# Two half-precision parts, one bias pass, and waits of GpSimd for VectorE's router operations

## The chip, the core and the metric

The kernel runs on one core of a Trainium2 chip. The core has TensorE (PE in the profile), VectorE (DVE), ScalarE (ACT), GpSimd (POOL) and SyncE (SP), each with its own instruction queue; they synchronize by semaphores. The metric is the device time of one launch in microseconds (us), the median over runs.

## What is computed

The input `x` is 16 images of 64 channels and 112x112 pixels, in f32. Cut to what matters:

```python
n  = layernorm over channels of x                     # per pixel
y  = sigmoid(conv3x3([max_c n, mean_c n]) + conv_b)   # one gate per pixel
x1 = x + n * y
t  = tokens of x1 (one per pixel, 64 values)
z  = layernorm(t)
p  = softmax(z @ router_w + router_b)                 # 8 experts
top_p, top_i = top_k(p, 2); top_p /= top_p.sum()
out = t + sum_k top_p[k] * (z @ expert_w[top_i[k]] + expert_b[top_i[k]])
```

The router bias and the expert biases are not zero in the inputs that are run.

## The kernel before, in words

Images go in 8 pairs (two images of 64 channels fill the 128 partitions). A pair has 14 steps of 8 image rows (896 pixels of each image). Three stages are software-pipelined over pairs: in a *round* r, stage A centres pair r and collects its channel maximum and sum of squares; stage B computes the square roots, the 3x3 convolution and the router for pair r-1; stage C applies the experts to pair r-2, with a lag of two steps. Rounds 2 to 7 have all three stages, round 8 has no A, rounds 9 and 10 have C alone. All queues are unrolled and written out by hand; each engine runs its own in order.

In C, the 18 numbers of a token (8 gates, 8 scaled gates, and two affine terms) lie in `q`. They must go through TensorE to be spread over channels, and TensorE reads them in bf16, so they are cut into three bf16 parts: ScalarE rounds `q` to the first (`part_one`), GpSimd subtracts it (`rest_one`), ScalarE rounds the rest to the second (`part_two`), and GpSimd subtracts again for the third (`part_three`). TensorE turns the parts (`turn`, L458), ScalarE copies the result to `s`. TensorE then spreads gates from `s` into PSUM `gb` (`spread`, L465) and the affine term into `tm` (`spread_a1`, L504), starts each of two accumulations `moe` with the biases (`biases`, L514: a pass with the high half `bh` of the bias, one with the low half `bl`), and adds the eight expert products (`experts`, L520). In each step six of eight gate multiplications are VectorE's (`scale_unit`, L662, reading PSUM) and two are GpSimd's (L1148, reading a copy that ScalarE made, L963). VectorE also adds `x1` (`finish`, L675); GpSimd forms it (`scale_x`, L1173).

VectorE's part of B is cut in *places*, two a step: place 2*step at the step's start, place 2*step+1 after the first half's work (`gate`). Places 1 to 3 and 7 to 9 hold Newton steps of the roots, 4 and 6 the convolution's input and the affine terms, 12 to 19 the router of the first half of the pixels, 20 to 27 that of the second. GpSimd has its part of B (`router`, `router_tail`) at a fixed point of each step, after `rest_one`. A *half step* below is one of the two halves that the queues of TensorE and VectorE are written in, each with one call of `biases`, three `scale_unit` on VectorE, one `finish` and, in rounds with A, one `channel_max` and one `centre_rows`.

Of the kernel before, what the change touches and what calls it, by code (L numbers as in the profile page):

```python
# [26 lines left out]
BF16 = mybir.dt.bfloat16  # L27
# [6 lines left out]
E = 8  # L34
P = 128
# [20 lines left out]
SR = SB + 3 * QN  # L56
QG, QB, QA, QM = 0, E, 2 * E, 2 * E + 1
# [13 lines left out]
B_POOL = ("lg_0", "bias_0", "lg_1", "bias_1", "m1_0", "m2_0", "qb_0", "qg_0", "m1_1", "m2_1", "qb_1", "qg_1")  # L71
# [4 lines left out]

def constant_arrays():

    f = np.zeros((P, CC + 3 * W + E + P), np.float32)
# [12 lines left out]
    f[:, o:o + E] = np.arange(E, 0, -1)  # L92
    o += E
    for part in range(3):
        for b in range(2):
            f[b * SB + part * QN + QM, o + b * CH:o + (b + 1) * CH] = -1.0
    g = np.zeros((P, (KT + 2) * P), np.float32)
    for part in range(3):
        for b in range(2):
            row = b * SB + part * QN  # L100
            for k in range(KT):
                for e in range(2):
                    lo = k * P + e * CH
                    g[row + QG + 2 * k + e, lo:lo + CH] = 1.0
            g[row + QA, KT * P + b * CH:KT * P + (b + 1) * CH] = 1.0
    g[:, (KT + 1) * P:] = np.eye(P)
    return f, g


def gated_expert_program(nc, x, conv_w, conv_b, router_w, router_b, expert_w, expert_b, const_f, const_g, out):  # L110
# [3 lines left out]
    with ExitStack() as ctx:  # L114
# [9 lines left out]
        cf = sb("cf", [P, CC + 3 * W + E + P])  # L124
        cg = sb("cg", [P, (KT + 2) * P], BF16)
# [9 lines left out]
        bias_base = cf[0:SR, bias_c:bias_c + P]  # L135

# [7 lines left out]
        bl = sb("bl", [SR, P], F16)  # L144
# [41 lines left out]
        res = sb("res", [W, 2, ROWS, 2 * QN])  # L186
        parts = sb("parts", [W, 2, ROWS, 2 * SB], BF16)
        s = sb("s", [P, 2, TOK], BF16)
# [11 lines left out]
        turn_out = tm[:, 1, :].bitcast(BF16)  # L200
# [25 lines left out]
        part2 = sem("part2")  # L226
        part3 = sem("part3")
# [13 lines left out]
        FIRST_LOADS, LOADS, BIAS_LOADS = 3 * 16, 5 * 16, 6 * 16  # L241
        POOL_SETUP = 5 + 1 + 6 * 5 + 1 + 2
# [71 lines left out]
        def part_of(v, n):  # L314

            return parts[:, v % 2, :, :].rearrange("w j (b k) -> w j b k", b=2)[:, :, :, n * QN:(n + 1) * QN]

        def by_part(t):
            return t.rearrange("w j (b k) -> w j b k", b=2)
# [14 lines left out]
        def _(sp):  # L334
# [66 lines left out]
            for part in range(3):  # L401
                for b in range(2):
                    row = b * SB + part * QN + QB
                    col = bias_c + b * CH
                    sp.dma_start(cf[row:row + E, col:col + CH], expert_b).then_inc(ld_bias, 16)
# [13 lines left out]
        def _(pe):  # L419
# [29 lines left out]
            def turn(r, step, v):  # L449

                if due(count := c_at(r, 1, v, 1)):
                    pe.wait_ge(part3, count)
                read_out(pe, r, step, 0)
                if due(count := c_at(r, 1, v - 1, 1)):
                    pe.wait_ge(a1_out, count)
                for j in range(ROWS):
                    for b in range(2):
                        last = pe.transpose(turn_out[b * SB:(b + 1) * SB, j * W:(j + 1) * W],  # L458
                                            parts[:, v % 2, j, b * SB:(b + 1) * SB], ident)
                last.then_inc(turned, 1)  # L460

            def spread(v, k, c, slot):
                for b in range(2):
                    rows = slice(b * SB, b * SB + 3 * QN)
# [44 lines left out]
            def biases(r, v, c):  # L509
                if due(count := c_at(r, 2, v - 1, c + 1)):  # L510
                    pe.wait_ge(final, count)
                for n, w in enumerate((bh, bl)):
                    for b in range(2):
                        pe.matmul(moe[b * CH:(b + 1) * CH, c, 0:HALF], w[:, b * CH:(b + 1) * CH],  # L514
                                  s[0:SR, v % 2, c * HALF:(c + 1) * HALF],
                                  start=(n == 0), stop=False, skip_group_check=True)
# [364 lines left out]
        def _(act):  # L881
# [168 lines left out]
            def body(r, A, Bp, steps=STEPS, tail=True):  # L1050
                for step in range(steps):
# [28 lines left out]
                    if parting:  # L1080
                        part_two(r, v + 2)
# [22 lines left out]
        def _(pool):  # L1104
# [26 lines left out]
            link(pool.tensor_tensor(bl[:, :], bias_base, bh[:, :], ALU.subtract))  # L1131
# [195 lines left out]
```

## Time and profile before

| | |
|---|---|
| median of 3 runs | 1491.57 us (1489.61 to 1493.1) |
| profiled execution | 1497.93 us, span 1496.1 us |
| busy in the span | TensorE 94%, VectorE 85%, GpSimd 73%, ScalarE 72% |
| mean granted TensorE clock | 0.963 of full |
| matmuls of the bias passes (L514) | 896 |
| all matmuls | 12198 |

The table is read from the profiled execution: the span runs from the first to the last instruction, and busy time is that in which an engine has an instruction in execution. A granted clock of 1.00 is TensorE's 2.4 GHz, 0.50 is 1.2 GHz.

### The profile page before, as it was taken

To read this page: it belongs to the slowest core of one execution; us is meant where nothing else is said; L and a number is where in the kernel's file an instruction comes from. 1 tells how busy PE (TensorE), PEld (TensorE's weight loads), DVE (VectorE), ACT (ScalarE), POOL (GpSimd) and SP (SyncE) were. 2 spreads that over 40 slices of the span, in tenths; PEclk is the share of its full clock that TensorE was granted. 3 is DMA by queue.
4 is the path that set the end of the run, shared out by engine and by line. 5 is a ranking of instruction groups with operands and counts; after the bars stand their busy time and mean duration, and the time that the engine had idled before them with its cause. 6 is when DMAs were issued, how large, how long until landed. Compare 5 with 4: busy or idle time off the path is not lost.

```text
span 1496.1 us, 34317 instructions
## 1 busy us (share of the span) xinstructions
PE 1402.2 (94%) x12198; PEld 660.5 (44%) x12198; DVE 1268.4 (85%) x1583; ACT 1080.0 (72%) x4061; POOL 1086.4 (73%) x729
## 2 busy tenths in 40 slices
PE   8854999999999999999999999999999889999998
PEld 8853444444444444444444444444444233333332
DVE  6787889988998889988898889988898788977776
ACT  6667788878887888878888788878888334444432
POOL 5234687868777787877788687876878678887765
PEclk9955999999999999999999999999999899999999
DMA  6442466656666566666656666666665356556563
GB/s 221 125 114 60 138 197 197 203 156 203 190 188 193 178 199 197 185 179 193 185 173 198 186 186 192 177 199 186 195 193 169 101 151 170 173 164 182 165 181 112
DMA packets 85851, 260.04 MB, mean 174 GB/s; under 512 B 13744, under 2 KB 13744, under 8 KB 85680
## 3 DMA queue, kind: packets, MB, share of 16 engines
q1 hardware_dynamic: 85680, 257.85, 57.7%
q8 instruction: 97, 1.59, 0.4%
q14 instruction: 74, 0.61, 0.1%
HBM read 206.41 MB, written 51.38 MB: 172 GB/s over the span
## 4 chain that ended last, share of the span: by engine, by line
PE 69%; DVE 9%; issue 7%; POOL 3%; ACT 3%; DVEq 0%; POOLq 0%; ACTq 0%
PE moe L520 39%; PE gb L465 13%; PE tm L444 8%; DVE gx L662 7%; PE moe L514 4%; PE tm L458 3%; PE tm L504 2%; POOL gx L1148 1%; PE tm L544 1%; POOL tt L1173 1%; ACT a1s L970 1%; ACT sq L919 1%; POOL parts L1162 1%; DVE stats L639 0%; ACT logit_mean L985 0%
## 5 line engine op out<-in xcount | busy, mean ns | idle before, releaser
L662 DVE TENSOR_TENSOR gx<-gb,xd 128x896 f32<-128x896 f32 x672 | 710.7, 1085 | 139.0 <-PE gb L465 135.6
L520 PE MATMUL moe<-gx,wc 128*64 128x448 f32 x3584 | 820.6, 558 | 0.0
L1148 POOL TENSOR_TENSOR gx<-gs,xd 128x896 f32<-128x896 f32 x224 | 486.2, 2170 | 302.1 <-ACT gs L963 291.6
L963 ACT ACTIVATE gs<-gb 128x896 f32<-128x896 f32 x224 | 205.3, 917 | 225.1 <-PE gb L465 225.0
L919 ACT ACTIVATE sq<-xct 112x64 f32<-112x64 f32 x1400 | 338.0, 244 | 8.1 <-DVE early_s L649 2.6
L520 PEld LDWEIGHTS moe<-gx,wc 128*64 128x64 f32 x3584 | 219.2, 137 | 244.0 <-issue 193.3
L465 PE MATMUL gb<-s,cg 54*128 54x448 bf16 x1792 | 261.4, 360 | 40.8 <-DVE gx L662 34.6
L919 ACT ACTIVATION_READ_ACCUMULATOR sq<-xct 112x1 f32 x1400 | 263.7, 188 | 0.0
L1173 POOL TENSOR_TENSOR tt<-xc,a1s 128x896 f32<-128x896 f32 x112 | 236.2, 2109 | 12.2 <-issue 10.5
L465 PEld LDWEIGHTS gb<-s,cg 54*128 54x128 bf16 x1792 | 57.0, 95 | 377.9 <-DVE gx L662 292.6
L444 PEld LDWEIGHTS tm<-rhs,xa 64*112 64x112 f32 x2800 | 175.1, 185 | 29.7 <-issue 11.5
L444 PE MATMUL tm<-rhs,xa 64*112 64x74 f32 x2800 | 171.7, 265 | 11.2 <-ACT logit_mean L904 8.4
L675 DVE TENSOR_TENSOR ot<-moe,tt 128x448 f32<-128x448 f32 x224 | 138.0, 616 | 31.5 <-PE moe L520 30.8
L900 ACT ACTIVATE xct<-tm 112x512 f32<-112x512 f32 x175 | 104.2, 595 | 61.2 <-PE tm L444 55.6
L970 ACT ACTIVATE a1s<-tm,ones 128x896 f32<-128x896 f32 x112 | 112.8, 1007 | 43.5 <-PE tm L504 43.5
L955 ACT ACTIVATE s<-tm 128x896 bf16<-128x896 bf16 x112 | 102.6, 916 | 11.9 <-PE tm L458 7.2
L639 DVE TENSOR_REDUCE stats<-xct 112x8 f32<-112x512 f32 x128 | 86.8, 678 | 18.3 <-ACT logit_mean L904 17.5
L1156 POOL TENSOR_TENSOR res<-q,parts 112x288 f32<-112x288 f32 x112 | 81.2, 725 | 9.7 <-ACT parts L942 9.7
L458 PEld LDWEIGHTS tm<-cg,parts 112*64 112x64 bf16 x1792 | 56.8, 111 | 67.7 <-POOL parts L1162 44.1
L1162 POOL TENSOR_TENSOR parts<-res,parts 112x288 bf16<-112x288 f32 x112 | 83.1, 742 | 0.1
L514 PE MATMUL moe<-s,bh 118*64 118x448 bf16 x448 | 80.8, 354 | 0.0
L639 DVE TENSOR_REDUCE early_s<-xct 112x8 f32<-112x512 f32 x96 | 65.1, 678 | 18.2 <-ACT early_l L904 17.3
(94 smaller groups left out, 1296.7 us busy)
## 6 DMA issues: line engine op xcount, KB each, us to landing
xd<-in_x_dram SPq DMA_DIRECT2D x448, 224.0 KB, 4.0
xa<-in_x_dram SPq DMA_DIRECT2D x112, 448.0 KB, 4.3
xc<-in_x_dram SPq DMA_DIRECT2D x112, 448.0 KB, 4.8
out_dram<-ot SPq DMA_DIRECT2D x112, 448.0 KB, 3.3
gx<-in_const_g_dram SPq DMA_DIRECT2D x1, 384.0 KB, 4.7
cf<-in_const_f_dram SPq DMA_DIRECT2D x1, 332.5 KB, 2.8
gx<-in_L_ffn_expert_w_dram SPq DMA_DIRECT2D x1, 128.0 KB, 4.5
cf<-in_L_ffn_expert_b_dram SPq DMA_DIRECT2D x6, 2.0 KB
```

Source lines behind the costliest of these rows:

```text
L444: last = pe.matmul(pair[:, b, j, :], xa[chans, step % XA, row * W:(row + 1) * W], rhs1[chans, :], start=True, stop=True)
L465: last = pe.matmul(gb[:, 2 * slot + b, 0:HALF], cg[rows, k * P:(k + 1) * P], s[rows, v % 2, c * HALF:(c + 1) * HALF], start=True, stop=True)
L514: pe.matmul(moe[b * CH:(b + 1) * CH, c, 0:HALF], w[:, b * CH:(b + 1) * CH], s[0:SR, v % 2, c * HALF:(c + 1) * HALF], start=(n == 0), stop= ...
L520: last = pe.matmul(moe[b * CH:(b + 1) * CH, c, 0:HALF], wc[:, k * CH:(k + 1) * CH], gx[:, u, b, :], start=False, stop=(k == KT - 1), skip_ ...
L639: dve.tensor_reduce(to[:, 0, lo + cols.start:lo + cols.stop], xct[:, step % 2, cols, :], AX.X, ALU.max) \
L662: dve.tensor_tensor(gx[:, i, :, :], gb[:, 2 * slot:2 * slot + 2, 0:HALF], xd[:, v % 2, :, c * HALF:(c + 1) * HALF], ALU.mult).then_inc(sca ...
L675: dve.tensor_tensor(ot[:, sl, cols], moe[:, c, 0:HALF], tt[:, sl, cols], ALU.add).then_inc(final, 1)
L919: last = act.activation(sq[:, n, :], xct[:, step % 2, n, :], ACT.Square, accum_out=to[:, 1, lo + n:lo + n + 1])
L963: act.activation(gs[:, j, :, :], gb[:, 2:4, 0:HALF], ACT.Copy).then_inc(gate_out, 1)
L970: act.activation(a1s[:, v % 2, :].rearrange("p (c t) -> p c t", c=2), tm[:, :, 0:HALF], ACT.Identity, bias=ones[:, :], scale=1.0).then_inc ...
L1148: pool.tensor_tensor(gx[:, ND + j, :, :], gs[:, j, :, :], xd[:, v % 2, :, j * HALF:(j + 1) * HALF], ALU.mult).then_inc(scaled_p, 1)
L1173: pool.tensor_tensor(tt[:, sl, :], xc[:, sl, :], a1s[:, sl, :], ALU.mult).then_inc(scaled_x, 1)
```

## The change

`q` is cut in two f16 parts instead of three bf16 parts: ScalarE's `part_one` and GpSimd's `rest_one` remain, `part_two` and `part_three` go. The 18 columns of a token are written out as two overlapping blocks of 13 columns (the eight gates and what follows them appear in both), so that a part has 26 rows and each gate stands twice; the bias matrix `bw` holds the high half of the bias at one copy of a gate and the low half at the other, so one pass of `biases` does what two did. GpSimd's scaled gates are written in two instructions, of 5 and 3 columns. GpSimd gets two more setup instructions and SyncE two more small bias loads. And ahead of each of its gate multiplications GpSimd waits until VectorE has ended the last operation of that half step's place (`vector_place`), where there is one.

```diff
 QN = 2 * E + 2
 SB = 64
-SR = SB + 3 * QN
-QG, QB, QA, QM = 0, E, 2 * E, 2 * E + 1
+G_LO = 5
+QB, QA, QM = G_LO, 2 * E, 2 * E + 1
+BLOCK, AGAIN = QB + E, QB
+PN = 2 * BLOCK
+SR = SB + 2 * PN
 D_PAIR = (0, 1, 3, 0, 1, 3)
 P_PAIR = 2
...
+        PLACE_END = {1: "y_a1", 2: "y_b1", 3: "r1", 4: "pool_mean", 6: "v2", 7: "y_a2", 8: "y_b2", 9: "rho"}
+        HALF_END = ("top", "ge", "key_max", "dl", "d", "ge2", "key_max2", "oh2")
+        for place in range(16):
+            PLACE_END[12 + place] = f"{HALF_END[place % 8]}_{place // 8}"
+
+        def vector_place(eng, r, place):
+
+            if 1 <= r <= PAIRS and place in PLACE_END:
+                b_done(eng, r, B_DVE, PLACE_END[place])
...
-            return parts[:, v % 2, :, :].rearrange("w j (b k) -> w j b k", b=2)[:, :, :, n * QN:(n + 1) * QN]
-
-        def by_part(t):
-            return t.rearrange("w j (b k) -> w j b k", b=2)
+            tokens = parts[:, v % 2, :, :].rearrange("w j (b k) -> w (j b) k", b=2)
+            return tokens[:, :, n * PN:(n + 1) * PN].rearrange("w t (i k) -> w t i k", i=2)
+
+        def q_blocks(v):
+
+            rows = q[:, v * ROWS:(v + 1) * ROWS, :]
+            return bass.AP(rows.tensor, rows.offset, [rows.ap[0], [QN, 2 * ROWS], [AGAIN, 2], [1, BLOCK]])
...
             def turn(r, step, v):
 
                 if due(count := c_at(r, 1, v, 1)):
-                    pe.wait_ge(part3, count)
+                    pe.wait_ge(rest1, count)
...
-                for n, w in enumerate((bh, bl)):
-                    for b in range(2):
-                        pe.matmul(moe[b * CH:(b + 1) * CH, c, 0:HALF], w[:, b * CH:(b + 1) * CH],
-                                  s[0:SR, v % 2, c * HALF:(c + 1) * HALF],
-                                  start=(n == 0), stop=False, skip_group_check=True)
+                for b in range(2):
+                    pe.matmul(moe[b * CH:(b + 1) * CH, c, 0:HALF], bw[:, b * CH:(b + 1) * CH],
+                              s[0:SR, v % 2, c * HALF:(c + 1) * HALF],
+                              start=True, stop=False, skip_group_check=True)
...
-                act.activation(part_of(v, 0), by_part(q[:, v * ROWS:(v + 1) * ROWS, :]), ACT.Copy) \
-                   .then_inc(part1, 1)
-
-            def part_two(r, v):
-                if due(count := c_at(r, 1, v, 1)):
-                    act.wait_ge(rest1, count)
-                act.activation(part_of(v, 1), by_part(res[:, v % 2, :, :]), ACT.Copy).then_inc(part2, 1)
...
-                    if parting:
-                        part_two(r, v + 2)
...
-            link(pool.tensor_tensor(bl[:, :], bias_base, bh[:, :], ALU.subtract))
+            link(pool.tensor_tensor(bias_base, bias_base, low_row.to_broadcast([SR, P]), ALU.mult))
+            link(pool.tensor_tensor(bh[:, :], bh[:, :], high_sign.to_broadcast([SR, P]), ALU.mult))
+            link(pool.tensor_tensor(bw[:, :], bias_base, bh[:, :], ALU.add))
...
             def rest_one(r, v):
                 if due(count := c_at(r, 1, v, 1)):
                     pool.wait_ge(part1, count)
-                if due(count := c_at(r, 1, v - 2, 1)):
-                    pool.wait_ge(part3, count)
-                pool.tensor_tensor(by_part(res[:, v % 2, :, :]), by_part(q[:, v * ROWS:(v + 1) * ROWS, :]),
-                                   part_of(v, 0), ALU.subtract).then_inc(rest1, 1)
-
-            def part_three(r, v):
-                if due(count := c_at(r, 1, v, 1)):
-                    pool.wait_ge(part2, count)
-                pool.tensor_tensor(part_of(v, 2), by_part(res[:, v % 2, :, :]),
-                                   part_of(v, 1), ALU.subtract).then_inc(part3, 1)
...
-                pool.tensor_tensor(q_tokens[:, rows, QG:QG + E], q_tokens[:, rows, QB:QB + E], wide(rho, rows),
+                rhos = wide(rho, rows)
+                pool.tensor_tensor(q_tokens[:, rows, 0:G_LO], q_tokens[:, rows, QB:QB + G_LO], rhos[:, :, 0:G_LO],
                                    ALU.mult).then_inc(b_pool, 1)
+                pool.tensor_tensor(q_tokens[:, rows, QB + E:QA], q_tokens[:, rows, QB + G_LO:QB + E],
+                                   rhos[:, :, G_LO:E], ALU.mult).then_inc(b_pool, 1)
...
                     cur, ahead, parting = on(r, v), on(r, v + 1), on(r, v + 2)
                     if cur:
+                        vector_place(pool, r, 2 * step)
                         scale_unit(r, v, 1)
                     if parting:
                         rest_one(r, v + 2)
@@ -1286,10 +1305,9 @@
                     if Bp:
                         router(r, step)
                     if ahead:
+                        vector_place(pool, r, 2 * step + 1)
                         scale_unit(r, v + 1, 0)
                         scale_x(r, v + 1)
-                    if parting:
-                        part_three(r, v + 2)
```

GpSimd's queue in rounds with all stages, from the multiplication at the start of step 0 to `scale_x` of that step and what follows (`gx<-gs,xd` is a gate multiplication, `tt<-xc,a1s` is `scale_x`, `e<-stats` feeds the first root; `b_dve` counts VectorE's operations of B). Before:

```order
L1148 TENSOR_TENSOR gx<-gs,xd 128x896 [waits mixed,gate_out]
L1156 TENSOR_TENSOR res<-q,parts 112x288 [waits part3,part1]
L1207 TENSOR_TENSOR dl<-oh,g 112x896 [waits b_act,b_dve]
L1237 TENSOR_TENSOR e<-stats,powers 112x224 [waits b_dve,joined,squared]
L1148 TENSOR_TENSOR gx<-gs,xd 128x896 [waits mixed,gate_out,ld_xd1]
L1173 TENSOR_TENSOR tt<-xc,a1s 128x896 [waits final,a1_out,ld_xc1]
L1162 TENSOR_TENSOR parts<-res,parts 112x16x18 [waits part2]
```

After:

```order
L1172 TENSOR_TENSOR gx<-gs,xd 128x896 [waits mixed,gate_out]
L1178 TENSOR_TENSOR parts<-q,parts 112x16x26 [waits part1]
L1222 TENSOR_TENSOR dl<-oh,g 112x896 [waits b_act,b_dve]
L1255 TENSOR_TENSOR e<-stats,powers 112x224 [waits b_dve,joined,squared]
L1172 TENSOR_TENSOR gx<-gs,xd 128x896 [waits gate_out,mixed,ld_xd1,b_dve]
L1188 TENSOR_TENSOR tt<-xc,a1s 128x896 [waits final,a1_out,ld_xc1]
```

The subtraction into `res` became one into `parts`, the second subtraction (`part_three`) is gone, and the multiplication behind `e<-stats` waits for `b_dve` too. The other multiplications behind a place of VectorE wait alike.

TensorE's queue in the second half of a step, with the two bias passes between the turned affine term and the expert products. The piece before:

```order
L504 MATMUL tm<-s,cg 64x448 x4
L514 MATMUL moe<-s,bh 64x448 x2
L514 MATMUL moe<-s,bl 64x448 x2
L520 MATMUL moe<-gx,wc 64x448 x2
L465 MATMUL gb<-s,cg 128x448 x4
L444 MATMUL tm<-rhs,xa 112x74 x8
```

and after:

```order
L535 MATMUL tm<-s,cg 64x448 x4
L544 MATMUL moe<-s,bw 64x448 x2
L550 MATMUL moe<-gx,wc 64x448 x2
L496 MATMUL gb<-s,cg 128x448 x4
L475 MATMUL tm<-rhs,xa 112x74 x8
```

Two of the four bias matmuls of a half step are gone; the rest keeps its order.

## Rows read from the trace of the kernel before

**Rows 1.** The page's busy time, share of the span and instructions of each engine.
```profile
PE 1402.2 (94%) x12198; PEld 660.5 (44%) x12198; DVE 1268.4 (85%) x1583; ACT 1080.0 (72%) x4061; POOL 1086.4 (73%) x729
```

**Rows 2.** Timeline of TensorE, 466 to 483, first bias pass: start, duration (us), line.
```profile
466.84 0.36 PE L514 MATMUL moe<-s,bh 118*64 118x448 bf16 x2
...
472.63 0.36 PE L514 MATMUL moe<-s,bh 118*64 118x448 bf16 x2
...
482.48 0.36 PE L514 MATMUL moe<-s,bh 118*64 118x448 bf16 x2
```

**Rows 3.** The chain of waits, 634 to 640: start, duration, what.
```profile
638.58 0.38 PE moe L514 x4
```

**Rows 4.** Groups by line and shape: busy us, mean ns | idle before, releaser.
```profile
L1173 POOL TENSOR_TENSOR tt<-xc,a1s 128x896 f32<-128x896 f32 x112 | 236.2, 2109 | 12.2 <-issue 10.5 <-ACT a1s L970 1.7
...
L1162 POOL TENSOR_TENSOR parts<-res,parts 112x288 bf16<-112x288 f32 x112 | 83.1, 742 | 0.1
L1156 POOL TENSOR_TENSOR res<-q,parts 112x288 f32<-112x288 f32 x112 | 81.2, 725 | 9.7 <-ACT parts L942 9.7
...
L948 ACT ACTIVATE parts<-res 112x288 bf16<-112x288 f32 x112 | 48.3, 431 | 0.0
```

**Rows 5.** Timeline, 577 to 584: a half step with place 18, and GpSimd beside it.
```profile
577.30 0.73 POOL L1162 TENSOR_TENSOR parts<-res,parts 112x288 bf16<-112x288 f32 x1
...
577.40 1.10 DVE L689 TENSOR_TENSOR key<-ge,prio 112x896 bf16<-112x896 bf16 x1
...
578.54 1.09 DVE L681 TENSOR_REDUCE key_max<-key 112x112 bf16<-112x896 bf16 x1
...
579.55 1.08 DVE L662 TENSOR_TENSOR gx<-gb,xd 128x896 f32<-128x896 f32 x1
...
583.69 0.61 DVE L714 TENSOR_TENSOR oh<-prio,ge 112x896 bf16<-112x896 bf16 x1
```

**Rows 6.** One line's instructions: duration ns min/median/max, first and last start.
```profile
L662 DVE TENSOR_TENSOR gx<-gb,xd x672: 1071/1083/1093, 144.2 to 1490.1; 128x896 f32<-128x896 f32 x168
```

**Rows 7.** Timeline, 643 to 648: step 0 of a round with all stages.
```profile
643.38 0.28 DVE L745 TENSOR_SCALAR p<-e 112x224 int32<-112x224 int32 x1 [0.65 <-POOL e L1237]
...
644.12 0.39 DVE L753 SCALAR_TENSOR_TENSOR u<-u,e 112x224 f32<-112x224 f32 x1
644.18 2.33 POOL L1148 TENSOR_TENSOR gx<-gs,xd 128x896 f32<-128x896 f32 x1 [0.84 <-issue]
...
644.55 2.21 DVE L756 SCALAR_TENSOR_TENSOR p<-u,p 112x224 f32<-112x224 f32 x1
...
647.82 0.93 PE L465 MATMUL gb<-s,cg 54*128 54x448 bf16 x4 [2.31 <-DVE gx L662]
```

**Rows 8.** Busy (count) of PE, PEld, DVE, ACT, POOL in two stretches; granted clock, DMA.
```profile
648.00:655.00 7.00, 7.00 (x36) 3.06 (x34) 5.24 (x8) 2.52 (x11) 1.38 (x2) 0.53 0.54 132
1200.00:1210.00 10.00, 7.82 (x48) 2.47 (x46) 9.63 (x14) 2.26 (x3) 5.94 (x5) 1.00 0.40 123
```

**Rows 9.** Timelines of VectorE and TensorE, 1154 to 1240, in round 8.
```profile
1160.25 2.22 DVE L753 SCALAR_TENSOR_TENSOR u<-u,e 112x224 f32<-112x224 f32 x1
...
1177.01 2.25 DVE L756 SCALAR_TENSOR_TENSOR r<-u,p 112x224 f32<-112x224 f32 x1
...
1202.16 0.55 PE L465 MATMUL gb<-s,cg 54*128 54x448 bf16 x4 [2.04 <-DVE gx L662]
...
1211.55 2.31 DVE L756 SCALAR_TENSOR_TENSOR p<-u,p 112x224 f32<-112x224 f32 x1
```

**Rows 10.** Timelines of GpSimd and VectorE, 602 to 609: step 11 of a round.
```profile
602.56 2.14 POOL L1148 TENSOR_TENSOR gx<-gs,xd 128x896 f32<-128x896 f32 x1 [0.86 <-ACT gs L963]
...
605.33 2.11 POOL L1216 TENSOR_TENSOR q<-lg,dl 112x896 f32<-112x896 f32 x1
...
607.36 0.61 DVE L697 TENSOR_TENSOR oh<-prio,ge 112x896 bf16<-112x896 bf16 x1
...
608.01 1.09 DVE L699 SCALAR_TENSOR_TENSOR dl<-oh,lg 112x896 f32<-112x896 bf16 x1
```

More of the change, by code:

```diff
@@ L70 @@
          + tuple(n + "_1" for n in HALF_ROUTER))
-B_POOL = ("lg_0", "bias_0", "lg_1", "bias_1", "m1_0", "m2_0", "qb_0", "qg_0", "m1_1", "m2_1", "qb_1", "qg_1")
+B_POOL = ("lg_0", "bias_0", "lg_1", "bias_1", "m1_0", "m2_0", "qb_0", "ql_0", "qg_0", "m1_1", "m2_1", "qb_1",
+          "ql_1", "qg_1")
 B_NORM = ("e1", "e2")
@@ L74, with gate_col, part_col @@
 GUESS = 0x5F3759DF
+def gate_col(e):
+    return e if e < G_LO else E + e
+def part_col(col):
+    return col if col < AGAIN else BLOCK + col - AGAIN
 def constant_arrays():
-    f = np.zeros((P, CC + 3 * W + E + P), np.float32)
+    f = np.zeros((P, CC + 3 * W + E + P + 2), np.float32)
     for b in range(2):
@@ L93, in constant_arrays @@
     o += E
-    for part in range(3):
+    f[:, o + P] = 1.0
+    for part in range(2):
         for b in range(2):
-            f[b * SB + part * QN + QM, o + b * CH:o + (b + 1) * CH] = -1.0
+            row = b * SB + part * PN
+            f[row + part_col(QM), o + b * CH:o + (b + 1) * CH] = -1.0
+            low = slice(row + part_col(QB), row + part_col(QB) + E)
+            f[low, o + P], f[low, o + P + 1] = -1.0, 1.0
     g = np.zeros((P, (KT + 2) * P), np.float32)
-    for part in range(3):
+    for part in range(2):
         for b in range(2):
-            row = b * SB + part * QN
+            row = b * SB + part * PN
             for k in range(KT):
@@ L103, in constant_arrays @@
                     lo = k * P + e * CH
-                    g[row + QG + 2 * k + e, lo:lo + CH] = 1.0
-            g[row + QA, KT * P + b * CH:KT * P + (b + 1) * CH] = 1.0
+                    g[row + part_col(gate_col(2 * k + e)), lo:lo + CH] = 1.0
+            g[row + part_col(QA), KT * P + b * CH:KT * P + (b + 1) * CH] = 1.0
     g[:, (KT + 1) * P:] = np.eye(P)
@@ L122, in sem @@
             return ctx.enter_context(nc.semaphore(name))
-        cf = sb("cf", [P, CC + 3 * W + E + P])
-        cg = sb("cg", [P, (KT + 2) * P], BF16)
+        cf = sb("cf", [P, CC + 3 * W + E + P + 2])
+        cg = sb("cg", [P, (KT + 2) * P], F16)
         gx = sb("gx", [P, UNITS, 2, HALF])
@@ L135, in gated_expert_program @@
         bias_base = cf[0:SR, bias_c:bias_c + P]
+        high_sign = cf[0:SR, bias_c + P:bias_c + P + 1]
+        low_row = cf[0:SR, bias_c + P + 1:bias_c + P + 2]
         cg_load = gx_flat[:, 0:(KT + 2) * P]
@@ L143, in gated_expert_program @@
         bh = sb("bh", [SR, P], F16)
-        bl = sb("bl", [SR, P], F16)
+        bw = sb("bw", [SR, P], F16)
         cwb = sb("cwb", [W, 18])
@@ L185, in gated_expert_program @@
         q = sb("q", [W, H, 2 * QN])
-        res = sb("res", [W, 2, ROWS, 2 * QN])
-        parts = sb("parts", [W, 2, ROWS, 2 * SB], BF16)
-        s = sb("s", [P, 2, TOK], BF16)
+        parts = sb("parts", [W, 2, ROWS, 2 * SB], F16)
+        s = sb("s", [P, 2, TOK], F16)
         gs = sb("gs", [P, NP, 2, HALF])
@@ L199, in gated_expert_program @@
         conv_out = tm[0:W, 0, 0:2 * H]
-        turn_out = tm[:, 1, :].bitcast(BF16)
+        turn_out = tm[:, 1, :].bitcast(F16)
         ld_first = sem("ld_first")
@@ L225, in gated_expert_program @@
         rest1 = sem("rest1")
-        part2 = sem("part2")
-        part3 = sem("part3")
         turned = sem("turned")
@@ L239, in gated_expert_program @@
         final = sem("final")
-        FIRST_LOADS, LOADS, BIAS_LOADS = 3 * 16, 5 * 16, 6 * 16
-        POOL_SETUP = 5 + 1 + 6 * 5 + 1 + 2
+        FIRST_LOADS, LOADS, BIAS_LOADS = 3 * 16, 5 * 16, 8 * 16
+        POOL_SETUP = 5 + 1 + 6 * 5 + 1 + 4
         def at(r, first, per, n):
@@ L400, in _ @@
             sp.wait_ge(ld_first, FIRST_LOADS)
-            for part in range(3):
+            for part in range(2):
                 for b in range(2):
-                    row = b * SB + part * QN + QB
-                    col = bias_c + b * CH
-                    sp.dma_start(cf[row:row + E, col:col + CH], expert_b).then_inc(ld_bias, 16)
+                    for first_row in (QB, part_col(QB)):
+                        row = b * SB + part * PN + first_row
+                        col = bias_c + b * CH
+                        sp.dma_start(cf[row:row + E, col:col + CH], expert_b).then_inc(ld_bias, 16)
             body(0, True)
@@ L463, in spread @@
                 for b in range(2):
-                    rows = slice(b * SB, b * SB + 3 * QN)
+                    rows = slice(b * SB, b * SB + 2 * PN)
                     last = pe.matmul(gb[:, 2 * slot + b, 0:HALF], cg[rows, k * P:(k + 1) * P],
@@ L941, in part_one @@
                         act.wait_ge(b_act, count)
-                act.activation(part_of(v, 0), by_part(q[:, v * ROWS:(v + 1) * ROWS, :]), ACT.Copy) \
-                   .then_inc(part1, 1)
-            def part_two(r, v):
-                if due(count := c_at(r, 1, v, 1)):
-                    act.wait_ge(rest1, count)
-                act.activation(part_of(v, 1), by_part(res[:, v % 2, :, :]), ACT.Copy).then_inc(part2, 1)
+                act.activation(part_of(v, 0), q_blocks(v), ACT.Copy).then_inc(part1, 1)
             def turned_to_sbuf(r, v):
@@ L1153, in rest_one @@
                     pool.wait_ge(part1, count)
-                if due(count := c_at(r, 1, v - 2, 1)):
-                    pool.wait_ge(part3, count)
-                pool.tensor_tensor(by_part(res[:, v % 2, :, :]), by_part(q[:, v * ROWS:(v + 1) * ROWS, :]),
-                                   part_of(v, 0), ALU.subtract).then_inc(rest1, 1)
-            def part_three(r, v):
-                if due(count := c_at(r, 1, v, 1)):
-                    pool.wait_ge(part2, count)
-                pool.tensor_tensor(part_of(v, 2), by_part(res[:, v % 2, :, :]),
-                                   part_of(v, 1), ALU.subtract).then_inc(part3, 1)
+                pool.tensor_tensor(part_of(v, 1), q_blocks(v), part_of(v, 0), ALU.subtract).then_inc(rest1, 1)
             def scale_x(r, v):
```

## The prediction, made before the changed kernel ran

> **What bounds the kernel now.** I read the busy shares first: TensorE stands at 94%, VectorE at 85%, GpSimd and ScalarE at 73% and 72% [rows 1]. Then I took the distance from one first bias pass to the next, which is the length of a half step. A free half step lasts 472.63 - 466.84 = 5.79 us, in which TensorE has no gap; the one that holds the end of step 0 lasts 482.48 - 472.63 = 9.85 us, 4.06 more [rows 2]. So TensorE bounds the free half steps, and the question for the others is what stopped it.
>
> The timeline of a half step of VectorE answers that. From place 18's first operation to place 19's it is 583.69 - 577.40 = 6.29 us, of which 579.55 - 577.40 = 2.15 is the place and 4.14 everything else [rows 5]. VectorE never idles in it, so it sets the pace: a half step lasts as long as the longer of TensorE's work (5.79) and 4.14 plus the place. A place up to 1.65 us is free now.
>
> The same rows show why places are long. `key` takes 1.10 us beside a GpSimd subtraction that began 0.10 before it (577.30) and lasts 0.73, and `oh`, of the same size, takes 0.61 with none beside it [rows 5]. In step 0 a Newton operation takes 2.21 us where a sister of its form takes 0.39, and it ends when the GpSimd multiplication of 644.18 has ended [rows 7]. VectorE's gate multiplications, which read PSUM and one tile, never show this: 1071 to 1093 ns over 672 of them [rows 6]. So a VectorE operation with two inputs in SBUF stands until a running GpSimd operation is through. The Trainium skill says so too (SBUF — State Buffer, Who interferes with whom: the second to issue fully blocks, when the VectorE instruction has two SBUF inputs and GpSimd's reads SBUF); by that rule the trace agrees, and it adds a warning: any GpSimd operation can block, the router's own as well as the gate multiplications that now wait.
>
> In step 0 this costs twice: TensorE stands 2.31 us [rows 7], and right after that its granted clock is 0.53, near 1.2 GHz, for 7 us [rows 8].
>
> **The bias pass.** Four bias matmuls take 0.38 us of the chain [rows 3]; two of them go, 0.19 us. There are 112 steps of two half steps, so 224 x 0.19 = 42.6 us if TensorE bounded all of them. The free half step becomes 5.60, and the place that VectorE can hold free falls from 1.65 to 1.46. The new operands change no matmul count elsewhere, and f16 beside bf16 is taken as equally fast, since the old pass already had f16 weights.
>
> **The parts.** Gone are 112 ScalarE copies of 0.43 and 112 GpSimd subtractions of 0.74. The subtraction that remains grows from 288 to 416 elements: between 0.73 at 288 and 2.11 at 896 [rows 4] the line gives 0.73 + 128 x 1.38 / 608 = 1.02; a cost in proportion gives 1.05. I take 1.0, so GpSimd does 0.28 more ahead of its router operation and 0.46 less in a step. ScalarE and GpSimd are covered by TensorE in nearly all steps, so this pays nothing by itself. Its bounds: none to 0.4 us a round at the one place where ScalarE is late. In the fill before round 2's first experts the chain from parts to the turned tile is two operations shorter; an estimate from those two durations is 1.2 us for each of two steps, I take 2 us in all (0 to 3). The two setup operations and the two bias loads lie beside the first centring matmuls and cost nothing; with that cover gone they would cost under 1 us. The scaled gates in two instructions cost GpSimd some 0.1 us, twice a round.
>
> **The waits in step 0.** GpSimd now multiplies only when place 1 has ended, so the Newton operation falls from 2.21 to 0.39, a gain of 1.82. But `e` comes 0.28 later (the longer subtraction is ahead of it), and VectorE already waits 0.65 for it [rows 7]. TensorE runs 0.38 earlier by then (two bias passes). Its stand of 2.31 becomes 2.31 - 1.82 + 0.28 + 0.38 = 1.15; with rounding in the queue I take 1.2 to 1.3. A stand of 2.04 left the clock at 1.00 [rows 8, 9], so this shorter one should leave it too. The excess over a free half step falls from 4.06 to 1.28, 2.8 us, in each of rounds 3 to 7: 13.9 us. Behind the waiting multiplication stands `scale_x` alone, which TensorE does not need, and the multiplication itself is used a half step and more later.
>
> **The waits in round 8.** Without centring work TensorE's half step is shorter, and four VectorE operations stand 2.2 to 2.3 us instead of 0.39, of which three are shown [rows 9]: 4 x 1.85 = 7.4. Two of the stands also lowered the clock; by the size in step 0 (4.06 less 2.31 is 1.75, some of it the place) I take 1.2 each, 2.4. Together 9.8 us.
>
> **What is given back.** The waits keep GpSimd's multiplications off VectorE's places, but not its router operations. Take step 11. Place 22 (`key`, `key_max`) ended 4.14 us before 607.36, at 603.2 [rows 5, 10], and without a block of its `key` (1.10 - 0.61 = 0.49, as place 18's [rows 5]) it ends at 602.7. GpSimd starts there, multiplies until 604.85, subtracts until 605.85 and adds gates for 2.1, until 607.95. VectorE is at place 23 4.14 us after place 22 ended, at 606.85, and its `oh` stands 1.1 us. Now place 23 is free of that (0.61 at 607.36) [rows 10]. Place 23 would last 0.61 + 1.0 + 1.05 = 2.65 instead of 1.65, and its half step 6.8 us, 1.2 over the new 5.60. The same holds for place 15 in step 7, another sum of 2.1 us; place 25 (two scaled-gate instructions) I put at 0.5, place 3 at 0.5. Places of 1.5 to 1.65 us (6, 9, 14, 18, 22, 26) are now over the free length by 0.1 to 0.25, 1.1 together, and place 12's half step keeps its 0.3, where GpSimd's own load is the limit. Sum outside step 0: 1.2 + 1.2 + 0.5 + 0.5 + 1.1 + 0.3 = 4.8 us a round. Before, by the same rule, it was about 2.6 (places 12, 14, 15, 18, 22 and 26 at 0.3 to 0.6 each, three of them the block of `key` that goes). So 2.2 to 2.4 a round is given back, for rounds 2 to 7 some 14 us, and 1.5 in round 8.
>
> **The sum**, against the profiled execution of 1497.9 us: 42.6 + 13.9 + 9.8 + 2 - 14 - 1.5 = 52.8 off, 1445.1. The median of the runs is 6.4 below that execution, of which 1.5 is one step 0 that ran longer than its sisters; so 1438 or 1439. I say 1438.
>
> **Rivals.**
> *The router operations do not block.* GpSimd's router operation ends before VectorE reaches the odd places. For it: VectorE's own idle time ahead of a place, which I set to none in steps 7 and 11. Against it: the 1.1 us worked out for step 11, which is long beside any such idle time (5.60 - 4.14 less a place). Then 14 + 1.5 + 3 come back: 1420.
> *The waits bring nothing.* VectorE's place 1 stays late because `e` is, TensorE stands over 2 us still and the clock falls. Then only the bias pass pays, less the places over the free length: 42.6 + 2 - 7 = 37.6, 1454. Against it is the 0.39 of the sister operation.
> *Slower: the two queues wait for one another.* VectorE stands behind a GpSimd router operation, ends its place late, GpSimd starts late and hits the next place too. If each of the eight odd router places stood a whole 2.1 us, and each cost 2.1 + 1.05 - 1.46 = 1.7 in its half step, in two router halves with their even places as well, it is 16 x 1.7 x 7 = 190 us, less the 68 gained above: about 1614. It makes the kernel slower than before from 0.6 us a place on. Against it: GpSimd's work in a step is 2 x 2.15 + 2.1 + 1.0 + 2.1 = 9.5 of 11.2 us, so it catches up within a step, and the even places wait for nothing of GpSimd's.
> *The wait is idle.* That GpSimd's count is met before it matters would leave all as the second rival; the 2.21 us operation says it is not met in step 0.
>
> **How the numbers follow.** Forecast 0.62, first rival 0.18, second with the idle wait 0.14, slower 0.03; the rest, 0.03, lies between the second rival and no change. The forecast alone holds 1430 to 1446. The range takes in the first rival and most of the second: 1415 to 1455. A measurement of this kernel tells 0.2% (3 us) from no change; faster by more than that has 0.96, within it 0.01, slower 0.03.
>
> **What would show it.** In the profile after: free half steps of 5.60 us; the Newton operation of step 0 at 0.39 and TensorE's stand there near 1.2 us at a granted clock of 1.00; in round 8 no VectorE operation above 1.7 us; `oh` at places 15 and 23 standing about 1 us behind GpSimd's sums; GpSimd's remaining subtraction at 1.0 us. The forecast is wrong if free half steps do not shorten, if the clock still falls in step 0, or if the matmuls with GpSimd's product begin to wait for it.

## The result, and the profile after

| | before | after |
|---|---|---|
| median | 1492.34 us (1489.61 to 1496.79, 4 runs) | 1444.57 us (1444.50 to 1445.11, 4 runs) |
| profiled execution | 1497.93 us | 1444.59 us |
| span | 1496.1 us | 1442.8 us |
| mean granted clock | 0.963 | 0.973 |

The ratio is 0.9684, 95% interval [0.9665, 0.9702]: 3.2% faster. Between the profiled executions 53.3 us went, against 52.8 in the forecast's sum; between the medians 47.8.

The page of the changed kernel, its busy shares, beside [rows 1]:

```profile
PE 1347.0 (93%) x11750; PEld 632.7 (44%) x11750; DVE 1271.4 (88%) x1583; ACT 1045.9 (72%) x3949; POOL 1039.1 (72%) x635
```

TensorE lost 448 matmuls and 55 us of busy time and is busy for nearly the same share as before; VectorE has the same 1583 instructions and nearly the same busy time, which in the shorter span is 88%. The two take turns as the bound.

TensorE's bias pass in the stretch with a step 0 (start, duration, line), as in [rows 2]:

```profile
621.68 0.36 PE L544 MATMUL moe<-s,bw 116*64 116x448 f16 x2
...
627.29 0.36 PE L544 MATMUL moe<-s,bw 116*64 116x448 f16 x2
...
634.08 0.36 PE L544 MATMUL moe<-s,bw 116*64 116x448 f16 x2
```

A free half step is 5.61 us, where it was 5.79, and the one of step 0 is 6.79, where it was 9.85. The timeline of all engines in that step 0, as in [rows 7]:

```profile
626.30 0.56 POOL L1255 TENSOR_TENSOR e<-stats,powers 112x224 f32<-112x224 f32 x1
...
626.89 0.28 DVE L775 TENSOR_SCALAR p<-e 112x224 int32<-112x224 int32 x1 [1.07 <-POOL e L1255]
...
628.06 0.39 DVE L786 SCALAR_TENSOR_TENSOR p<-u,p 112x224 f32<-112x224 f32 x1
...
628.53 2.14 POOL L1172 TENSOR_TENSOR gx<-gs,xd 128x896 f32<-128x896 f32 x1 [1.67 <-ACT a1s L994]
...
629.51 0.55 PE L496 MATMUL gb<-s,cg 52*128 52x448 f16 x4 [1.11 <-DVE gx L692]
```

GpSimd's multiplication starts when the last Newton operation has ended (628.45), not while it waits; that operation takes 0.39 us instead of 2.21. What remains is VectorE's wait of 1.07 us for `e`, and TensorE stands 1.11 us for it. The releaser named for GpSimd (`a1s`) is not the last one: the new wait is on VectorE, and that is the instruction that ended just before. The clock of that stretch, beside the 0.53 of [rows 8] (busy of PE, PEld, DVE, ACT, POOL; granted clock; DMA):

```profile
630.00:636.00 6.00, 6.00 (x72) 3.05 (x68) 5.75 (x9) 4.80 (x21) 4.68 (x3) 1.00 0.59 153
```

What was given back shows in step 11, as in [rows 10] (timeline of GpSimd and VectorE):

```profile
585.27 1.09 DVE L711 TENSOR_REDUCE key_max<-key 112x112 bf16<-112x896 bf16 x1
...
586.43 2.14 POOL L1172 TENSOR_TENSOR gx<-gs,xd 128x896 f32<-128x896 f32 x1 [1.69 <-ACT parts L972]
...
588.53 0.97 POOL L1178 TENSOR_TENSOR parts<-q,parts 112x416 f16<-112x416 f32 x1
...
589.46 2.09 POOL L1231 TENSOR_TENSOR q<-lg,dl 112x896 f32<-112x896 f32 x1
...
590.41 1.62 DVE L727 TENSOR_TENSOR oh<-prio,ge 112x896 bf16<-112x896 bf16 x1
```

The multiplication starts when `key_max` has ended (586.36), the sum of gates (L1231) lands on place 23, and `oh` takes 1.62 us instead of 0.61. The half steps by place, from the distances between bias passes in a middle round (us):

| half step holding | before | after |
|---|---|---|
| place 1 (step 0) | 9.8 (once 11.3) | 6.79 |
| place 3 | 5.81 | 6.20 |
| place 14 | 6.43 | 6.20 |
| place 15 | 6.10 | 6.81 |
| place 22 | 6.27 | 5.87 |
| place 23 | 5.82 | 6.81 |
| place 25 | 5.81 | 5.64 |
| place 26 | 6.27 | 6.02 |
| a free one | 5.80 | 5.61 |

By stages (distances between the same bias passes of the two profiled executions): the fill up to the first one became 2.8 us shorter, round 2 (whose bias passes begin at step 2) 2.5, rounds 3 to 7 5.7 to 5.8 each and 7.3 where step 0 had been 11.3, round 8 11.0, and what follows up to the end 6.9. Together that is the 53.3.

### The profile page after: what moved, and what is told of

Its sections match the earlier page's. It is cut to its first block, busy times and chain, and to the rows that moved or that the text cites. A ratio compares the mean times of both kernels' runs of the same rounds, so it can differ in the third digit from the quotient of the medians.

```text
span 1442.8 us, 33190 instructions
## 1 busy us (share of the span) xinstructions
PE 1347.0 (93%) x11750; PEld 632.7 (44%) x11750; DVE 1271.4 (88%) x1583; ACT 1045.9 (72%) x3949; POOL 1039.1 (72%) x635
## 4 chain that ended last, share of the span: by engine, by line
PE 61%; DVE 19%; issue 9%; POOL 2%; ACT 1%; DVEq 0%; POOLq 0%; ACTq 0%
PE moe L550 35%; DVE gx L692 12%; PE gb L496 12%; PE tm L475 7%; PE tm L535 2%; PE moe L544 2%; PE tm L489 2%; DVE oh L727 2%; PE tm L574 1%; DVE ot L705 1%; DVE u L781 1%; POOL dl L1222 1%; DVE stats L669 1%; DVE early_s L669 0%; ACT gs L987 0%
## 5 line engine op out<-in xcount | busy, mean ns | idle before, releaser
L550 PE MATMUL moe<-gx,wc 128*64 128x448 f32 x3584 | 811.4, 552 | 0.0
L1172 POOL TENSOR_TENSOR gx<-gs,xd 128x896 f32<-128x896 f32 x224 | 479.9, 2142 | 298.7 <-ACT gs L987 135.8
L496 PE MATMUL gb<-s,cg 52*128 52x448 f16 x1792 | 259.0, 356 | 47.8 <-DVE gx L692 40.4
L496 PEld LDWEIGHTS gb<-s,cg 52*128 52x128 f16 x1792 | 56.9, 94 | 384.9 <-DVE gx L692 330.7
L475 PEld LDWEIGHTS tm<-rhs,xa 64*112 64x112 f32 x2800 | 172.0, 183 | 31.7 <-issue 17.6
L1178 POOL TENSOR_TENSOR parts<-q,parts 112x416 f16<-112x416 f32 x112 | 108.0, 964 | 10.2 <-ACT parts L972 10.2
L979 ACT ACTIVATE s<-tm 128x896 f16<-128x896 f16 x112 | 102.5, 916 | 0.4 <-PE tm L489 0.4
L489 PEld LDWEIGHTS tm<-cg,parts 112*64 112x64 f16 x1792 | 59.9, 111 | 56.4 <-issue 56.4
L544 PE MATMUL moe<-s,bw 116*64 116x448 f16 x448 | 80.9, 354 | 0.0
L489 PE MATMUL tm<-cg,parts 112*64 112x112 f16 x1792 | 64.1, 214 | 1.4 <-ACT early_l L934 1.3
```

The lines of the kernel that those rows point to most:

```text
L475: last = pe.matmul(pair[:, b, j, :], xa[chans, step % XA, row * W:(row + 1) * W], rhs1[chans, :], start=True, stop=True)
L550: last = pe.matmul(moe[b * CH:(b + 1) * CH, c, 0:HALF], wc[:, k * CH:(k + 1) * CH], gx[:, u, b, :], start=False, stop=(k == KT - 1), skip_ ...
L1172: pool.tensor_tensor(gx[:, ND + j, :, :], gs[:, j, :, :], xd[:, v % 2, :, j * HALF:(j + 1) * HALF], ALU.mult).then_inc(scaled_p, 1)
```

## The experiments

Times are medians; the ratio is to the kernel before on the same chip.

### The waits alone, and everything but the waits

`waits_only` is the kernel before with `vector_place` and its two calls. `no_waits` is the changed kernel with

```diff
-            if 1 <= r <= PAIRS and place in PLACE_END:
+            if False:
```

> The kernel before with the waits of GpSimd for VectorE's places added, and nothing else (three bf16 parts, two bias passes). Theory (each wait removes a block of VectorE in step 0 and round 8, and moves GpSimd's router operation onto the next odd place): step 0 loses about 3.5 us of its 4.06 us excess in five rounds, round 8 about 10 us, and places 15 and 23 stand some 0.4 and 0.65 us longer in seven rounds (7 us): 1472 us, and the half step at place 23 goes from 5.80 to about 6.4. Rival (the waits bring nothing, all comes from the bias pass): 1490 to 1493.

> The changed kernel without the waits. Theory: step 0 has its 2.2 us Newton operation back, TensorE stands about 3 us and its clock falls, round 8 has its four long operations: 1455 us (1450 to 1462), and oh at place 23 still stands about 0.8 us since the router operation comes 0.3 earlier only. Rival (the waits bring nothing): 1444 to 1446.

| | 3 parts, 2 passes | 2 parts, 1 pass |
|---|---|---|
| no waits | 1492.7 | 1499.6, ratio 1.0058 [1.0036, 1.0079] |
| waits | 1481.5, ratio 0.9927 [0.9912, 0.9942] | 1444.6, ratio 0.9684 [0.9665, 0.9702] |

Neither half of the change brings alone what was expected: the waits alone take 11 us off, the parts and the one pass alone make the kernel 7 us slower, and together they take 48 off. In `waits_only` step 0's half step is 6.37 us and that of place 23 is 6.56, both near what the theory had; between the spans of the profiled executions 18.0 us went (expected 20.5), and the rest of the miss is the distance of the profiled execution before from its median, as below.

`no_waits` was mispriced by both theories. Its bias passes around a step 0:

```profile
642.64 0.36 PE L544 MATMUL moe<-s,bw 116*64 116x448 f16 x2
...
656.00 0.36 PE L544 MATMUL moe<-s,bw 116*64 116x448 f16 x2
...
661.60 0.36 PE L544 MATMUL moe<-s,bw 116*64 116x448 f16 x2
...
671.22 0.36 PE L544 MATMUL moe<-s,bw 116*64 116x448 f16 x2
```

13.36 us where there were 9.85, and two half steps later 9.62 where there were 5.8. The timeline of VectorE, GpSimd and TensorE in it:

```profile
642.57 0.39 DVE L781 TENSOR_TENSOR u<-p 112x224 f32<-112x224 f32 x1
...
642.62 2.34 POOL L1172 TENSOR_TENSOR gx<-gs,xd 128x896 f32<-128x896 f32 x1 [0.40 <-issue]
...
642.99 2.21 DVE L783 SCALAR_TENSOR_TENSOR u<-u,e 112x224 f32<-112x224 f32 x1
...
644.92 2.21 POOL L1188 TENSOR_TENSOR tt<-xc,a1s 128x896 f32<-128x896 f32 x1
...
645.24 2.14 DVE L786 SCALAR_TENSOR_TENSOR p<-u,p 112x224 f32<-112x224 f32 x1
...
648.44 0.93 PE L496 MATMUL gb<-s,cg 52*128 52x448 f16 x4 [4.68 <-DVE gx L692]
```

The multiplication now starts beside the second of place 1's four operations instead of the third, so the third stands until it ends. That one is served between the multiplication and `scale_x`, which follows without a gap, and the fourth stands behind `scale_x`. Two blocks instead of one, and TensorE stands 4.68 us instead of 2.31.

The kernel before already had this case in round 8, where TensorE's half step is shorter (5.36 us) for want of centring work. Behind the operation of 1160.25 in [rows 9] its timelines go on with

```profile
1162.50 2.14 DVE L756 SCALAR_TENSOR_TENSOR p<-u,p 112x224 f32<-112x224 f32 x1
...
1165.70 0.93 PE L465 MATMUL gb<-s,cg 54*128 54x448 bf16 x4 [4.50 <-DVE gx L662]
```

and that half step took 11.63 us. So it could be read before any run that shorter half steps bring a second block; the next experiment shows that the faster TensorE is enough for it.

### One pass with three parts

```diff
-                for n, w in enumerate((bh, bl)):
+                for n, w in enumerate((bh,)):
```

> The kernel before (three bf16 parts, no waits) with the first bias pass only; it leaves out the pass with the low half of the biases. Theory (the faster TensorE lets GpSimd start its multiplication of step 0 earlier against VectorE's Newton steps, so two of them are blocked instead of one): step 0's half step goes from 9.8 to 12 us or more, and the whole to 1485 to 1500 us, though 448 matmuls are gone. Rival (the two f16 parts, whose longer subtraction makes the root's input late, are what costs 7 us without waits): step 0's half step stays near 10 and the time is about 1492.7 - 22 = 1471, or down to 1455.

1487.9 us, ratio 0.9975 [0.9963, 0.9986]. The kernel leaves out the low half of the biases. Step 0's half step is 11.7 to 12.6 us in its six rounds (in the profiled execution before: 9.8 to 11.6). So in step 0 the faster TensorE is enough, without the longer subtraction, to move GpSimd's multiplication onto two Newton operations:

```profile
637.06 0.39 DVE L751 TENSOR_TENSOR u<-p 112x224 f32<-112x224 f32 x1
...
637.38 2.08 POOL L1148 TENSOR_TENSOR gx<-gs,xd 128x896 f32<-128x896 f32 x1 [0.67 <-issue]
...
637.49 2.22 DVE L753 SCALAR_TENSOR_TENSOR u<-u,e 112x224 f32<-112x224 f32 x1
...
639.43 2.22 POOL L1173 TENSOR_TENSOR tt<-xc,a1s 128x896 f32<-128x896 f32 x1
...
639.75 2.15 DVE L756 SCALAR_TENSOR_TENSOR p<-u,p 112x224 f32<-112x224 f32 x1
```

Half of the 896 bias matmuls gone, and 3 us gained. Without the waits a faster TensorE is worth next to nothing here. It does not explain all of `no_waits`, though, which is another 12 us slower. At place 3 the last Newton operation takes 2.2 to 2.3 us in each of rounds 3 to 7 of `no_waits` and 0.39 here, and the half step 8.0 to 11.1 us against 5.9, together 18 us, of which other places give part back. So without waits the two parts cost time, while with them they save 15 us (next section). In round 5 of `no_waits` GpSimd's multiplication starts 0.13 us ahead of that operation, here 0.11 us behind it; which of the differences between three parts and two makes those 0.24 us was not tried. In `no_waits`:

```profile
661.58 2.15 POOL L1172 TENSOR_TENSOR gx<-gs,xd 128x896 f32<-128x896 f32 x1 [0.58 <-ACT gs L987]
...
661.71 2.27 DVE L786 SCALAR_TENSOR_TENSOR r<-u,p 112x224 f32<-112x224 f32 x1
```

### The second pass put back

The changed kernel with a further pass of zero weights `bz` behind the first.

```diff
-                for b in range(2):
+                for w in (bw, bz):
+                    for b in range(2):
```

> The changed kernel with a second bias pass of zero weights behind the first, so that TensorE has its old count of bias matmuls. Theory (TensorE bounds only half steps of 5.8 us or less, VectorE the rest): free half steps return to 5.80, the longer ones (about 8 in a round: steps 0 and 1, places 14, 15, 18, 22, 23, 25 and 26) stay; about 170 of 224 half steps lose 0.19 us, 1477 us. Rival (TensorE bounds all): 1444.6 + 42.6 = 1487.

1466.5 us, ratio 0.9829 [0.9815, 0.9844]. With the waits the pass is worth 21.9 us, half of 224 x 0.19. Both theories were too high, the first by 10: in more half steps than it counted VectorE is the bound, and some are longer with one pass than with two (step 0 6.79 against 6.60 us, place 3 6.20 against 6.01, place 26 6.02 against 5.87). With two passes place 15's half step is 6.81 us, exactly as with one. `second_pass` against `waits_only` is two parts against three with the same two passes: 15.0 us between the medians, 13.5 between the spans. In a middle round it is 1.5 us: the half steps of places 18, 22 and 26 become 0.5 shorter each, since `key` takes 0.6 to 0.7 us there instead of 1.2, those of place 14 and ahead of place 12 0.3 each, and places 1, 15 and 23 become 0.25 longer each. The spans thus divide into 18.0 us for the waits, 13.5 for the parts and 21.8 for the pass, in this order; in another order the shares are others, as `no_waits` and `one_pass_three_parts` show.

### The router waits

The changed kernel, waits at places 1 to 9 only.

```diff
-            if 1 <= r <= PAIRS and place in PLACE_END:
+            if 1 <= r <= PAIRS and place in PLACE_END and place < 12:
```

> The changed kernel with the waits at places 1 to 9 only, none at the router places 12 to 27. Theory (the router waits remove little, since key_max ends only shortly after the gate copy is there, and push GpSimd's sum onto places 15 and 23): 1439 to 1444, places 15 and 23 at about 6.5 instead of 6.81 us. Rival (the router waits pay too): 1448 or more.

1445.5 us, ratio 0.9683 [0.9664, 0.9703]: level with the changed kernel. In rounds 3 to 7 places 15 and 23 are at 6.35 and 6.49 us, as the theory had it, and a round is 1.0 us shorter. But round 8 has two half steps of 12.4 and 11.1 where there were 6.3 and 6.7. One operation of place 13 there (timeline, VectorE and GpSimd):

```profile
1183.14 0.98 POOL L1178 TENSOR_TENSOR parts<-q,parts 112x416 f16<-112x416 f32 x1
...
1183.80 7.08 DVE L714 TENSOR_TENSOR ge<-lg,top 112x896 bf16<-112x896 f32 x1
...
1184.06 1.77 POOL L1201 TENSOR_TENSOR lg<-logit_mean,rho 112x896 f32<-112x896 f32 x1
...
1185.76 2.15 POOL L1172 TENSOR_TENSOR gx<-gs,xd 128x896 f32<-128x896 f32 x1
...
1187.84 2.10 POOL L1188 TENSOR_TENSOR tt<-xc,a1s 128x896 f32<-128x896 f32 x1
```

It stands through four GpSimd operations in a row and runs when the last has ended (1189.94). With the router waits the multiplication behind `L1201` waits for this `ge`, which ends the row. In the changed kernel:

```profile
1190.10 2.95 DVE L714 TENSOR_TENSOR ge<-lg,top 112x896 bf16<-112x896 f32 x1
...
1193.13 2.14 POOL L1172 TENSOR_TENSOR gx<-gs,xd 128x896 f32<-128x896 f32 x1 [1.03 <-DVE ge L714]
```

So the router waits cost 1 us in a round with all stages and save 8.3 in round 8 (10.4 in these two half steps, 2.2 of it given back in others). Neither theory had that.

### One wait, at place 1

```diff
-            if 1 <= r <= PAIRS and place in PLACE_END:
+            if 1 <= r <= PAIRS and place == 1:
```

> The changed kernel with one wait a round, at place 1 (step 0), and none elsewhere. Theory (without waits GpSimd's multiplication and the one behind it block two Newton operations of place 1, TensorE stands 4.7 us and its clock falls; place 3 has a block of its own): the half step of step 0 falls from 12 to 13.4 back to 6.8 us in six rounds, that of place 3 stays at 8.0 or more, and round 8's place 13 keeps its 12.6: about 1499.6 - 6 x 5.9 = 1464 us. Rival (the block at place 3 only follows from the late place 1): place 3 falls to 6.2 too and the time to about 1450.

1461.0 us (1455.1 to 1467.5), ratio 0.9791 [0.9749, 0.9833]. Step 0 is at 6.79, place 3's half step at 7.9 to 9.6, and round 8 keeps its 12.46, as the theory had them. Between the medians this one wait takes 39 us off the 1499.6, though these runs spread over 12; the others take the remaining 16. Place 1 holds a step of the roots: most of what the waits bring is not won at the router's places, which the title names.

### GpSimd's addition in another step

```diff
-                elif step == 7:
+                elif step == 8:
                     logits_biased(r, 1)
```

> The changed kernel with GpSimd's addition of the router bias for the second half of the pixels in step 8 instead of step 7 (nothing else of GpSimd's router is in step 8). Theory (oh at place 15 stands because this addition runs): the half step at place 15 falls from 6.81 to about 5.8, the one at place 17 rises from 5.64 to about 6.1, net 0.5 us in seven rounds: 1441 us. Rival (place 15 is long by itself, a matter of VectorE's own work): place 15 stays at 6.8 and the time at 1444 to 1448.

1440.3 us, ratio 0.9659 [0.9637, 0.9681]. Place 15's half step fell from 6.81 to 5.82, place 17's rose from 5.64 to 6.04. The block goes where the addition goes (timeline of step 8):

```profile
552.84 2.09 POOL L1209 TENSOR_TENSOR lg<-lg,brb 112x896 f32<-112x896 f32 x1
...
553.90 1.98 DVE L714 TENSOR_TENSOR ge<-dl,top 112x896 bf16<-112x896 f32 x1
```

### GpSimd's router tail one step later

```diff
-                if step == 0:
-                    second_gates(r, 1)
-                elif step == 1:
-                    summed_gates(r, 1)
-                elif step == 2:
-                    scaled_gates(r, 1)
+                if step == 1:
+                    second_gates(r, 1)
+                elif step == 2:
+                    summed_gates(r, 1)
+                    scaled_gates(r, 1)
```

> The changed kernel with GpSimd's router tail one step later (the second gates in step 1, their sum and scaling in step 2), so that in step 0 the operation that feeds the first root has no 1.7 us operation ahead of it. Theory (TensorE's stand in step 0 is now VectorE's wait for that operation): the step 0 half step falls from 6.79 to about 5.65, place 3's from 6.20 to about 5.9, in six rounds: 1436 us. Rival (the stand is the Newton steps' own length): 1443 to 1446.

1435.0 us, ratio 0.9623 [0.9601, 0.9645]. Step 0's half step is 5.64, place 3's 5.84. In step 0 `e` is now ready before VectorE asks for it (timeline):

```profile
621.33 0.59 POOL L1255 TENSOR_TENSOR e<-stats,powers 112x224 f32<-112x224 f32 x1
...
621.88 0.68 DVE L669 TENSOR_REDUCE early_s<-xct 112x8 f32<-112x512 f32 x1
...
622.48 0.27 DVE L775 TENSOR_SCALAR p<-e 112x224 int32<-112x224 int32 x1
```

### Both, with earlier ends of the waits

Both moves, and waits of the router places end earlier: at `key` instead of `key_max`, and there is none at the first place of each half, which holds only `top`, a reduction with one input.

```diff
-        HALF_END = ("top", "ge", "key_max", "dl", "d", "ge2", "key_max2", "oh2")
-        for place in range(16):
+        HALF_END = (None, "ge", "key", "dl", "d", "ge2", "key2", "oh2")
+        for place in (n for n in range(16) if HALF_END[n % 8]):
```

> The two moves together, and the waits for a router place end at its last operation with two inputs in SBUF (key instead of key_max, none for place 12). Theory: the gains add, and places 15 and 23 stand about 0.3 less: 1431 us (1428 to 1435). Rival (GpSimd's router operations block elsewhere as much): 1436 to 1440.

1426.9 us (1426.7 to 1427.1), ratio 0.9568 [0.9547, 0.959], the best version found, 17.7 us under the changed kernel and 1 us below the expected range. The two moves alone took 4.3 and 9.6, so the earlier ends bring about 4. `oh` at place 23 takes 1.25 us instead of 1.62, its half step 6.45.

## Why the prediction held, and where not

**The bias pass, 42.6 us.** The free half step was to be 5.60 us; measured 5.61. As a worth of the pass the 42.6 is not borne out: put back into the changed kernel it costs 21.9, and taken from the kernel before it brings 3. The waits, which the sum has at 13.9 + 9.8 - 14 - 1.5 = 8.2 if all that is given back is put down to them, are worth 11 when added first and 55 when added last.

**Step 0, 4.06 us of excess down to 1.28.** Measured 6.79 - 5.61 = 1.18; the stand of 1.2 us and the clock at 1.00 were as stated. That `e` would come later and leave just this stand is confirmed by moving what is ahead of it: the stand went.

**The parts, subtraction at 1.0 us.** Measured 0.96. "This pays nothing by itself" is the sentence that failed: two parts instead of three are worth 15 us where waits and passes are equal. Three of the blocks that `part_three` lays on `key` were in the working, but booked as something that lessens what is given back, not as a gain of the parts. The half step ahead of place 12, where 0.3 us was to stay, has gone from 6.11 to 5.64.

**Given back: 1.2 us at places 15 and 23, 0.5 at 3 and 25.** Measured 1.20, 1.20, 0.59 and 0.03 over a free half step. The size holds, the cause only in part: without any wait at a router place the two are at 6.35 and 6.49 us, so of the 1.20 the router waits make 0.46 and 0.33, and the rest stands without it. Place 25 went otherwise: its `ge` began at the end of the first of the two scaled-gate instructions and ran ahead of the second, which stood instead (timeline of the changed kernel):

```profile
601.77 1.24 POOL L1238 TENSOR_TENSOR q<-q,rho 112x560 f32<-112x560 f32 x1
...
602.83 1.12 DVE L714 TENSOR_TENSOR ge<-dl,top 112x896 bf16<-112x896 f32 x1
...
602.97 1.71 POOL L1240 TENSOR_TENSOR q<-q,rho 112x336 f32<-112x336 f32 x1
```

GpSimd was later by that, and `key` of place 26 stood 0.26 us behind `scale_x`: 0.41 over instead of the 0.25 forecast. Place 14 is 0.6 over, not 0.1 to 0.25; that was already so before (6.43), and VectorE waits 0.32 us for ScalarE there. All places but 1 and 4 together are 5.1 us over in a round, where they were 2.7: 2.4 given back, as forecast.

**Round 8: 9.8 - 1.5 + 28 x 0.19 = 13.6 us.** Measured 11.0. "No VectorE operation above 1.7 us" is wrong: a `ge` takes 2.95 us and an `oh` 2.20. Set against round 9, whose half steps hold nothing of B, the places that gained gained 12.6 us rather than 9.8 (the working counted four long operations and missed a fifth, the 2.14 above), but those that lost gave back 7.8, not 1.5; the free length took 6.1 where 5.3 was forecast. The term was sized from rounds with centring work, whose longer half steps leave GpSimd more room; that this is the reason is argued, not tried.

**The sum** was right to 0.5 us against the profiled execution, and that close it was by luck, with errors of opposite sign: 2.6 too much in round 8, 0.8 too little in the fill and as much in rounds 9 and 10, and the 1.5 of the one long step 0, which fell away too. In rounds 3 to 7, which are most of the time, it is sound: 5.8 a round forecast, 5.7 to 5.8 measured.

**From the sum to the median.** The forecast was 1438, the time 1444.6, and nearly all of that comes from subtracting 6.4 us, by which the profiled execution lay above the median. That distance belonged to the kernel before: its runs spread over 8 us (1488.4 to 1496.8), those of the changed kernel over 0.6. All kernels here that keep stands of 2 us and more spread over 3 to 12 us, those without over 0.4 to 1.7. What varies with the time is the clock: the mean granted clock is 0.967 to 0.969 in the twelve fastest of the 26 runs of the kernel before beside the experiments, up to 1491.3 us, and 0.963 and 0.964 in the two longest, 1496.3 and 1496.4. The profiled execution, at 0.963, is of that kind. And the same stand sometimes lowers the clock and sometimes not: in the profile of `wait_at_place_1_only` TensorE stands 2.26 us at place 3 in round 4 and again in round 5, and the stretches right behind the two are (as in [rows 8])

```profile
479.00:485.00 6.00, 6.00 (x70) 3.05 (x68) 5.42 (x9) 4.75 (x20) 2.40 (x2) 1.00 0.60 154
646.00:652.00 6.00, 6.00 (x48) 2.58 (x46) 4.71 (x7) 3.70 (x13) 0.91 (x1) 0.76 0.60 153
```

Their half steps took 7.94 and 9.56 us.

**The rivals.** *The router operations do not block* is refuted by the move of the addition. *The waits bring nothing* was priced at 1454; with no waits at all the time is 1499.6. Its place was right and its price far off, since the blocks of [rows 7] were left as they were while everything around them moved. *Slower, the queues wait for one another* did not come: no half step with a router place is more than 1.2 us over in the rounds with all stages. *The wait is idle* is refuted by step 0's timeline after, where the multiplication starts only behind the last Newton operation, and by the 39 us of that one wait.

## What to carry to other kernels

An engine that is made faster shifts when others start. Here that alone ate up nearly all that the removed pass saved (3 us left), and with the two parts on top it became a loss of 7; price a removed matmul with the operations that will then run side by side, and look for a stretch of the old trace in which the engine is already that fast, as round 8 here. Where two engines block one another, let the one with slack wait for the other, and look at what it runs right behind the operation that waits, since a row of operations can hold the other engine for all of its length. Read how long a blocked operation takes against its free sister of the same form, and place long optional work where the other engine has no operation with two inputs in SBUF.

## What the runs showed of the hardware

A VectorE operation that stands behind a GpSimd operation is not always served when that one ends and another follows without a gap. `ge` took 7.08 us through four of them (1.08 free), and 2.95 through two in the changed kernel; the third Newton operation of `no_waits` and the `ge` of place 25 were served between two. What decides was not tried and stays open. TensorE stands of 1.1 us, and of up to 1.57 in round 8 of the changed kernel, left the granted clock at 1.00; of stands of 2.26 us one lowered it and one did not, as above. The stretch that holds the end of the stand of 4.68 us in `no_waits` and what follows had a mean granted clock of 0.66:

```profile
645.00:655.00 10.00, 6.56 (x34) 2.99 (x36) 8.22 (x11) 2.05 (x12) 2.13 (x1) 0.66 0.35 90
```
